# Storing a step's sums by four transfers instead of one, in the edge loop of a graph layer

## The reference, cut to what matters

```python
def _L0_gnn_ref(x, W, a_src, a_dst, edge_W, edge_b, bias, edge_attr, edge_index):
    h = (x @ W.T).reshape(n, H, D)                       # 6250 nodes, 8 heads of 32
    h_src, h_dst = h[src], h[dst]                        # 200000 edges, sorted by dst
    alpha = einsum('ehd,hd->eh', h_src, a_src) + einsum('ehd,hd->eh', h_dst, a_dst)
    enc = relu(edge_attr @ edge_W.T + edge_b).reshape(-1, H, D)
    alpha = leaky_relu(alpha + sum(enc * h_dst, -1), 0.2)
    ex = exp(alpha - segment_max(alpha, dst)[dst])
    attn = ex / segment_sum(ex, dst)[dst]
    return segment_sum(h_src * attn[..., None], dst).reshape(n, H * D) + bias
x = x + _L0_gnn_ref(layernorm(x), ...)
x = x + _L0_ffn_ref(layernorm(x), ...)                   # two experts of a routed feed-forward layer
```

## Time and profile before

| | |
|---|---|
| median of 3 runs (lowest to highest) | 4180.87 us (4165.67 to 4185.18) |
| the profiled execution | 4159.17 us |
| its span, first to last instruction | 4157.4 us |
| PE busy | 2392.0 us, 58% |
| DVE busy | 2354.5 us, 57% |
| POOL busy | 2016.2 us, 48% |
| ACT busy | 992.1 us, 24% |
| mean granted clock of PE | 0.734 of full speed |
| the store's issues, all on SP | 110, 528.0 KB each |

### The profile page before, as it was taken

One profiled execution on the slowest core, in us unless ns is written; L12 is line 12 of the kernel. 1 busy time (PEld: TensorE's weight loads), 2 busy tenths in 40 slices (PEclk: granted clock), 3 DMA queues, 4 the chain that ended last, 5 costly groups with the idle time before them and its releaser, 6 DMA issues. The chain is left out here.

```text
span 4157.4 us, 45593 instructions
## 1 busy us (share of the span) xinstructions
PE 2392.0 (58%) x8886; PEld 1609.8 (39%) x8886; DVE 2354.5 (57%) x3523; ACT 992.1 (24%) x3079; POOL 2016.2 (48%) x2041
## 2 busy tenths in 40 slices
PE   3300556566566565565565665665656656416998
PEld 2200334333343343343343343433433433204887
DVE  7596556556556565565565565565655555443223
ACT  4300222222222222222222222222222222124332
POOL 2411555565555555555555655655556555244200
PEclk9755677776777777777777777767767777656999
DMA  7201444444444444444444444444444498320000
GB/s 240 76 30 46 114 125 115 124 124 115 125 122 118 125 123 120 126 122 118 124 115 124 126 117 124 124 113 125 117 122 124 115 118 113 52 66 23 13 20 29
DMA packets 322416, 437.60 MB, mean 105 GB/s; under 512 B 115526, under 2 KB 257832, under 8 KB 322132
## 3 DMA queue, kind: packets, MB, share of 16 engines
q0 software_dynamic: 90000, 262.14, 25.6%
q1 hardware_dynamic: 231540, 174.91, 14.8%
q10 hardware_dynamic: 848, 0.26, 0.0%
HBM read 351.33 MB, written 85.74 MB: 105 GB/s over the span
## 5 line engine op out<-in xcount | busy, mean ns | idle before, releaser
L856 POOL DMA_INDIRECT src_in<-t_node_rows,rec_in x1760 | 1800.8, 1023 | 1369.2 <-DVE weighted L1077 806.8
L1032 DVE SCALAR_TENSOR_TENSOR prod<-p_enc,near 128x512 f32<-128x512 f32 x880 | 566.4, 685 | 1224.6 <-ACT near L963 734.1
L904 PE MATMUL p_sum<-weighted,hot 128*128 128x264 f32 x3520 | 1021.8, 453 | 34.4 <-DVE weighted L1077 34.2
L871 PE MATMUL p_pick<-ident,hot 128*128 128x128 f32 x440 | 162.6, 370 | 1310.6 <-ACT hot L947 883.0
L904 PEld LDWEIGHTS p_sum<-weighted,hot 128*128 128x128 f32 x3520 | 794.5, 229 | 284.5 <-issue 114.6
L871 PEld LDWEIGHTS p_pick<-ident,hot 128*128 128x128 f32 x440 | 68.5, 156 | 1467.8 <-ACT hot L947 1011.1
L1036 DVE TENSOR_REDUCE dots<-prod 128x32 f32<-128x1024 f32 x440 | 536.9, 1220 | 15.2
L885 PE MATMUL p_pick<-win,hotT 128*128 128x272 f32 x880 | 439.9, 593 | 160.3 <-issue 119.6
L1077 DVE TENSOR_TENSOR weighted<-src_in,weighted 128x1024 f32<-128x1024 f32 x440 | 521.8, 1226 | 0.4 <-ACT weighted L969 0.4
L963 ACT COPY near<-p_pick 128x272 f32<-128x272 f32 x440 | 169.9, 386 | 1246.6 <-remote 726.1
L982 ACT COPY sums<-p_sum 128x264 f32<-128x264 f32 x440 | 166.9, 379 | 780.7 <-PE p_sum L904 524.7
(11 more groups left out here) (293 smaller groups left out, 1639.5 us busy)
## 6 DMA issues: line engine op xcount, KB each, us to landing
win<-t_node_rows SPq DMA_DIRECT2D x440, 136.0 KB
t_block_sums<-sums SPq DMA_DIRECT2D x110, 528.0 KB
src_in<-t_node_rows,rec_in POOLq DMA_INDIRECT x1760
attrT<-t_block_attr SPq DMA_DIRECT2D x330, 36.0 KB
flags_in<-t_block_flags SPq DMA_DIRECT2D x440, 4.0 KB
t_node_rows<-out_rows SPq DMA_DIRECT2D x49, 136.0 KB, 1.7
x<-in_x SPq DMA_DIRECT2D x4, 1536.0 KB, 25.7
out_x<-x SPq DMA_DIRECT2D x48, 128.0 KB
```

What stands on the lines that cost most here:

```text
L856: pool.indirect_dma_start(src[:, q.par, b, k, :], None, scr["rows"], bass.IndirectOffsetOnAxis(ap=rec_i[:, q.par, b, k:k + 1], axis=0)).th ...
L871: nc.tensor.transpose(p_hotT, hot[:, q.par, b, :], keep["ident"][:, :]).then_inc(s["turned"], 1)
L904: last = nc.tensor.matmul(p_sum[b % 2][:, 0:ROW], hot[:, q.par, b, :], weighted[:, b, k, :], start=(k == 0), stop=(k == W - 1))
L1032: nc.vector.scalar_tensor_tensor(prod[:, b % 2, 2 * half:2 * half + 2, :], p_enc[(PAIRS * b + half) % len(p_enc)][:, :, :], 0.0, near[:, q ...
```

## The change

The store becomes four DMAs, one for each block (128 pieces of 1056 bytes, 132 KB), each after a wait for that block's sums alone. Blocks 0 and 1 are stored after the loads of the same step, blocks 2 and 3 at the start of the next body, where the one store stood, ahead of the loads. The counts that ACT and the end of the loop wait for are multiplied by Q.

```diff
-            def store(q):
-                sp.wait_ge(s["sums"], Q * q.s + Q)
-                rows = scr["sums"][0:BLOCKS * P, :].rearrange("(n q p) e -> n p q e", q=Q, p=P)
-                v = rows[q.s, :, :, :] if isinstance(q.s, int) else rows[bass.ds(q.s, 1), :, :, :].rearrange("o p q e -> (o p) q e")
-                sp.dma_start(v, sums[:, q.par, :, :]).then_inc(s_stored[q.par], 16)
+            def store(q, b):
+                sp.wait_ge(s["sums"], Q * q.s + b + 1)
+                rows = scr["sums"][0:BLOCKS * P, :].rearrange("(n q p) e -> n q p e", q=Q, p=P)
+                v = rows[q.s, b, :, :] if isinstance(q.s, int) else rows[bass.ds(q.s, 1), b, :, :].rearrange("o p e -> (o p) e")
+                sp.dma_start(v, sums[:, q.par, b, :]).then_inc(s_stored[q.par], 16)
...
             def body(q):
                 if q.since(1):
-                    store(q.prev())
+                    for b in range(Q // 2, Q):
+                        store(q.prev(), b)
                 load(q.next().next())
+                for b in range(Q // 2):
+                    store(q, b)
 
             def last():
-                for k in (STEPS - 2, STEPS - 1, STEPS):
-                    store(straight(k - 1))
+                for b in range(Q // 2, Q):
+                    store(straight(STEPS - 3), b)
+                for k in (STEPS - 2, STEPS - 1):
+                    for b in range(Q):
+                        store(straight(k), b)
                 for one in s_stored:
-                    sp.wait_ge(one, 16 * STEPS // RING)
+                    sp.wait_ge(one, 16 * Q * STEPS // RING)
...
                 if q.since(RING):
-                    act.wait_ge(s_stored[q.par], 16 * q.turn)
+                    act.wait_ge(s_stored[q.par], 16 * Q * q.turn)
```

## The result

The change is slower, by little: 4197.02 us, the median of 15 runs (4188.62 to 4209.18, and one of 6940 us, which the ratio leaves out), against 4170.43 us (4163.17 to 4185.18, 15 runs), ratio 1.0062, 95% interval 1.0051 to 1.0074. The forecast was no change, 4180 us, and the measurement is outside it. The profiled execution took 4202.46 us, 43.3 more than the one before: 26.6 are the difference of the medians, the rest is where the two profiled ones lie in their groups.

The account below looks back on a forecast made before the run. POOL's gather ring bounds the kernel: 20.95 + 2.3 (end of crawl) + 5.0 (held-up work) = 28.3 us a step. Cost 0, gain 0, drain -1: 4158 us profiled, 4180 us as median; own range 4160 to 4201, overall 3860 to 4330.

Parts of the forecast that it names:

- The ring: POOL's gathers of a step, around which the loop turns: gathers 20.95 + end of the crawl 2.3 + held-up work 5.0 = 28.3 us.
- the crawl: Part of a step in which all the program's engines stand or move slowly; said to end 2.3 us after the last gather.
- 5.0 us of held-up work: From `near` of block 2 through DVE's weighing to the gathers' restart: work that the crawl has delayed, 5.0 us a step.
- Cost: 0: Three more DMA issues a step on SP, about 1.3 us plus 0.3, hidden under SP's 812.3 us of waiting for sums.
- By this reading the load of a step is the same 512 pieces: `rec_in`'s 512 pieces come at the same place, starting the crawl at the latest 3.4 us after block 3's store.
- Any burst among them tips it: Gathers load what engines' hand-overs need nearly to its limit; any burst starts the crawl, lasting until about the gathers' end.
- Gathers stop at the same moment, and the ring stays 20.95 + 2.3 + 5.0. Gain: 0: POOL's step stays unchanged because the crawl still starts before `near` of block 2, 3.4 us against 4.1; no time saved.
- the middle term: End of the crawl: `near` of block 2 comes 2.3 us after the last gather.
- the crawl starts earlier (slower): Stores among the gathers start the crawl 1.8 us or more ahead; 138 us more, 4320 us, or 4510; chance 0.28.
- Its signs: Slower rival's signs: `near` of block 1 over 8 us after block 3's store, POOL idling 9 us or more.
- too late, or not at all (faster): `near` of block 2 slips through under gathers: 3840 or 4075 us, far bound 3404 without POOL's 7.33 us idling; chance 0.38.
- The rule of the Trainium skill: Fixed cost of about 2 us per DMA: three more, taken serially, 6 us a step, some 660 us; judged off the path.

Follow-up runs that it names:

- r2: Kernel before with `rec_in`'s 512-piece load issued four times, three into a buffer nobody reads; second chip, 4245.21 us in one run (before 4250.63).
- s4: Kernel before with no store in the loop, all 110 issued behind it, ACT not waiting for stores; second chip, 4416.73 us in one run (before 4242.36).
- e2: Kernel before with the whole store issued behind the loads instead of ahead; chip without the crawl, 3422.42 us, ratio 0.9992.
- e1: Change with all four stores written ahead of the loads, SP's order the same as the change's; chip without the crawl, 3431.4 us, ratio 1.0002.
- x1: e1 with one wait for all four sums, then four single-block stores, none early; another chip without the crawl, ratio 1.0003.
- y1: x1 unchanged, once more, on yet another chip without the crawl; ratio 1.0002 (before 3424.76 us).
- s1: e1 unchanged, once more, on the second chip, with the crawl; 4357.74 us, ratio 1.027 against the kernel before.

## Why the prediction was wrong, point by point

- **The ring**, gathers + end of the crawl + 5.0 us of held-up work: right, and it carries every run with the crawl. In the table `near` of block 2 plus 5.0 us is the step in all ten rows with the crawl.
- **"Cost: 0" for three more issues on SP, hidden**: as work of SP this holds, as it still waits 650 us for sums. As a disturbance of others it doesn't. It is the term that failed: +0.50 us a step in the two profiles on the first chip, 0.25 by the medians (26.6 us), and 1.1 to 1.2 us a step on the second (117 and 123 us). What the runs show in its place: the three transfers go out 3.6, 5.5 and 9.9 us behind the gathers' start, ahead of the crawl, and afterwards `near` of block 1 comes 1.7 us later (2.7 us on the second chip). Through what they delay it stays open.
- **"By this reading the load of a step is the same 512 pieces"**: refuted. r2 has four times as many and is the kernel before; s4 has none near and crawls at the same point. The rows had it already: `near` of block 1 is 1.1 us late at 2009.74, 0.1 us behind the issue of `rec_in`, so what starts 2.4 us behind `rec_in` can't be what made it late; and in 88 of 96 steps of that trace some register or wait instruction of SP takes 0.6 us or more before `rec_in` is issued. It was read from one place where two things coincided: at the start of the loop the gathers had been going for 8 us when the crawl began. **"Any burst among them tips it"**: s4 has neither the store's 512 pieces nor `rec_in`'s there and crawls as before, and e2's stretch at a DMA share of 0.91, on another chip, doesn't crawl. Only the four small flag loads of s4 are left of it.
- **"Gathers stop at the same moment, and the ring stays 20.95 + 2.3 + 5.0. Gain: 0"**: the gathers' end stayed (21.06 us), the middle term didn't: 2.50 us became 3.02, and on the second chip 3.17 us became 4.3 to 4.4. I had taken it as a constant that doesn't react to how late `near` of block 1 is, from 7.1 to 7.4 us at four places. In fact it does react, beyond a slack: it takes the whole front of block 2 with it. By the means of the table, against the first row, `near` of block 1 1.7 us later goes with a step 0.5 us longer, 4.6 to 4.8 us later with 1.8 to 1.9 us. The one in five longer steps were the sign of it in the trace before, and I used them only for the rival.
- **The rival "the crawl starts earlier (slower)"**: right in its direction and in the longer step made the rule, wrong in its mechanism. It wanted the crawl to start 1.8 us or more ahead; PE slows down at 12 to 13 us behind the start in all of them, and block 3's sums are only 0.1 to 0.25 us later in the means. Its price of 1.3 us in 106 steps is what the second chip shows, 117 and 123 us for 138; the first chip had a third of it by the profiles (43.3 us) and a fifth by the medians, since there one step in two is still short. Its signs were set too far out: on the first chip `near` of block 1 came 5.9 us behind block 3's sums, not over 8 us behind its store, and POOL idled 8.0 us, not 9 (on the second chip 8.5 to 8.8 us behind the sums, and 9.3 to 9.4 us).
- **The rival "too late, or not at all (faster)"** had the largest chance, and nothing of it came. Its far bound, 3404 us for a loop without any idling, is nearly what the chips without the crawl show (3427, 3416 and 3425 us), but with the kernel before as well: it is a property of the occasion, and no store brings it about.
- **The rule of the Trainium skill** on a DMA's fixed cost ("DMA: Bandwidth & Descriptors", section "Anatomy of one DMA"): the page gives its figure for transfers issued from GpSimd, and these are SP's. Three more transfers are free on a chip without the crawl (e1, in the change's own order, 1.0002; x1 1.0003), as I had argued. With it they cost 0.25 to 1.2 us a step together, where the serial estimate was 6. Neither bears out a cost per transfer.

That the forecast lies only 17 us from the measured median is luck in part: on the second chip the same change costs 117 to 123 us.

## What to carry to other kernels

A wait with no releaser in the program ("remote") in the middle of a step may be a condition of the chip; before explaining it by the nearest transfer, look for a step in which that transfer isn't there. Transfers that nobody waits for need not be free: here a store in four pieces cost 0.6% on one chip, 2.7 to 2.9% on another and nothing on three (e1; x1 and y1, with all four at once), so one larger transfer was the safe side. That isn't a price for each transfer (r2 has three more for nothing), and an experiment that moves an instruction must be checked against the order that the engine then sees: e1 and s1 changed nothing in it. And a term that looks constant over most steps has a slack inside: the steps that don't fit (here one in five) tell how much of it is left.

## What the runs showed of the hardware

- One program runs at 3416 to 3427 us on three chips and at 4242 to 4251 us on another, 24% apart, each within 0.7% of its median. On the chip of the first result it was 4170 us.
- Where it is slow, PE's matmuls fall from 16 in 3 us to none, 12 to 13 us behind the first of 16 back-to-back gathers, at a DMA share of 0.43; where it is fast, 96 steps of the same gathers stand back to back, 0.30 us apart, and nothing stops. The second chip was slow twice and each other one was met once, so whether it is the chip or what else ran at that time isn't shown, nor why it takes 12 us.
- In the crawl 1536 more pieces a step have no measurable effect (r2, one run), and taking out the store, with `rec_in` and the attributes moved away, gains nothing (29.38 us a step for 29.26), while splitting a store in four, with three of the parts sent ahead of the crawl, costs 1.1 to 1.2 us a step. Why adding hurts when taking away doesn't help is open, and so is what the crawl waits for.
